# The first layer's experts in 40 steps instead of 47: whole tiles of one expert and mixed tiles of two experts' ends

## The reference

```python
# xn = layernorm(x): 1024 tokens x 256
logits = xn @ router_weight.T + router_bias            # 16 experts
top_val, top_idx = top_k(logits, 4)                    # 4 experts per token: 4096 rows in all
top_val = softmax(top_val)
gate_up = einsum('th,ehd->etd', xn, gate_up_proj) + gate_up_proj_bias   # per expert 256 x 512
gate, up = gate_up[..., ::2], gate_up[..., 1::2]
gate = minimum(gate, 7.0); up = clip(up, -7.0, 7.0)
glu = gate * sigmoid(gate * 1.702)
out = einsum('etd,edh->eth', (up + 1.0) * glu, down_proj) + down_bias   # per expert 256 x 256
out = (out * router_scores.T[:, :, None]).sum(axis=0)
x = x + attention(xn) * silu(out)
# second layer: linear attention, and 32 experts of 96 columns with a shared expert
```

## Time and profile before

| what | value |
|---|---|
| median of 3 runs | 425.56 us (424.31 to 426.42) |
| span of the profiled execution, first to last instruction | 422.5 us |
| what lies around the span, by the median | 3.06 us |
| PE busy | 407.8 us, 97% of the span |
| DVE busy | 330.4 us, 78% |
| first-layer tile loop on PE | about 39.0 to 176.5 us |

### The profile page before, as it was taken

The page is one execution under the profiler, slowest core; times in us unless marked ns, Lnnn a source line. Parts: engine busy times, 40 slices in busy tenths (PEclk is TensorE's granted clock), DMA queues, the critical chain, the costliest instruction groups (busy, mean ns, idle before and its releaser), DMA issues.

```text
span 422.5 us, 10072 instructions
## 1 busy us (share of the span) xinstructions
PE 407.8 (97%) x3213; PEld 321.5 (76%) x3213; DVE 330.4 (78%) x1121; ACT 233.1 (55%) x592; POOL 216.9 (51%) x208
## 2 busy tenths in 40 slices
PE   8999999999999999989999989999999999999995
PEld 4856999999999999856766668548877786565684
DVE  5876899999987666678999999847688774545896
ACT  3273233333433454589999972554777766633731
POOL 2114487888842322067786720067877740577710
PEclk9899999999999999969999999999999999999999
DMA  6947688889999998729977978023556553333322
GB/s 222 393 167 266 196 265 268 289 256 311 297 316 286 303 314 277 216 62 245 193 152 176 226 269 294 1 67 97 170 182 188 178 173 101 111 101 103 99 62 74
DMA packets 42275, 84.17 MB, mean 199 GB/s; under 512 B 7137, under 2 KB 27105, under 8 KB 41585
## 3 DMA queue, kind: packets, MB, share of 16 engines
q1 hardware_dynamic: 30656, 60.99, 44.1%
q0 software_dynamic: 9936, 20.85, 19.6%
q10 hardware_dynamic: 1632, 1.71, 1.2%
HBM read 65.81 MB, written 15.60 MB: 193 GB/s over the span
## 4 chain that ended last, share of the span: by engine, by line
PE 89%; DVE 7%; issue 2%; DMA 1%; ACT 1%; ACTq 0%; DVEq 0%
PE ps L1173 20%; PE ps L1189 9%; PE ps L1124 7%; PE ps L1370 7%; PE ps L1293 5%; PE ps L1151 5%; PE ps L1268 4%; PE ps L952 3%; PE ps L968 3%; PE ps L1381 3%; PE ps L1110 3%; PE ps L1162 2%; PE ps L971 2%; PE ps L941 2%; PE ps L1338 2%
## 5 line engine op out<-in xcount | busy, mean ns | idle before, releaser
L549 POOL DMA_INDIRECT til<-xn_rows,gidx x71 | 70.7, 996 | 86.4 <-PE ps L1162 38.9
L1173 PEld LDWEIGHTS ps<-til,experts 128*128 128x128 f32 x752 | 91.0, 192 | 3.7 <-issue 1.5
L1173 PE MATMUL ps<-til,experts 128*128 128x128 f32 x752 | 91.8, 275 | 0.1
L714 ACT ACTIVATE til<-ps 128x256 f32<-128x256 f32 x47 | 18.0, 383 | 69.8 <-PE ps L1162 69.8
L839 ACT ACTIVATE til<-til,mxs 128x128 f32<-128x128 f32 (+1 forms) x128 | 49.0, 452 | 0.0
L1189 PE MATMUL ps<-experts,til 128*128 x188 | 48.4, 381 | 0.0
L762 ACT ACTIVATE til<-ps,wtile 128x256 f32<-128x256 f32 x95 | 42.0, 468 | 3.7 <-PE ps L1153 2.4
L1795 DVE CUSTOM_DVE_ANT_0 til<-ps,cst 128x128 f32<-128x128 f32 (+1 forms) x128 | 37.8, 351 | 5.2 <-PE ps L1268 4.4
L1189 PEld LDWEIGHTS ps<-experts,til 128*128 128x128 f32 x188 | 32.1, 190 | 2.8 <-issue 0.3
L600 POOL DMA_INDIRECT rou<-sorted_rows,slotu x16 | 20.5, 1283 | 25.8 <-DMA sorted_rows<-til 19.4
L1126 PE MATMUL ps<-xn,til 128*64 128x192 f32 x192 | 33.8, 329 | 0.0
(11 more groups left out here) (247 smaller groups left out, 936.8 us busy)
## 6 DMA issues: line engine op xcount, KB each, us to landing
experts<-in_gu SPq DMA_DIRECT2D x47, 512.0 KB, 5.4
sorted_rows<-til SPq DMA_DIRECT2D x95, 128.0 KB, 1.9
experts<-in_gu SPq DMA_DIRECT2D x8, 768.0 KB
experts<-in_dn SPq DMA_DIRECT2D x4, 1024.0 KB, 12.4
experts<-in_dn SPq DMA_DIRECT2D x8, 384.0 KB
experts<-att SPq DMA_DIRECT2D x44, 32.0 KB
til<-xn_rows,gidx POOLq DMA_INDIRECT x71
xr<-in_x SPq DMA_DIRECT2D x2, 512.0 KB, 4.2
```

Of the source, the lines that this page charges most:

```text
L549: po.indirect_dma_start(to, None, xn_dram[s.n], bass.IndirectOffsetOnAxis(ap=gidx[:, t:t + 1], axis=0))\
L1173: mm = pe.matmul(ps[:, b0, m * P:(m + 1) * P], gw[:, j, k * w + m * P:k * w + (m + 1) * P], xgT[:, j % 2, k, :], start=(k == 0), stop=(k = ...
```

## The change

The first layer's experts are padded to 64 rows instead of 128. The whole pairs of 64 rows make 32 tiles of one expert (`WHOLE0`). What an expert has left over, at most 64 rows, is a half tile, and two of those stand side by side in each of 8 mixed tiles (`MIXED0`). The loop has 40 steps: four whole tiles with a mixed one as the fourth of each five. The weights lie in six slots (four in `big` and two in `att`), and a mixed tile fills two of them. It has its own path on each engine: the rows are the stationary operand, 64 columns of the array per expert; the bias comes in as a matmul; DVE gates rows instead of columns (`gate_rows`), PE turns the result back (`turn_rows_back`), ACT copies it (`copy_rows`), and ACT copies the second expert's down weights ahead (`copy_other_down`). The routing gets more DVE instructions. The fixed tile numbers are new: rotations after gathers 5, 8, 10, 13, 15, 18, 20 and 23, heads in SP's steps 14 to 24 and 25 to 35, the value columns after gathers 27 and 37, bias weights from tile 19, bias rows from 28. `weights_ahead` stays at five before the number of tiles, which is step 35 now. Some semaphores are merged into the engines' chains.

```diff
-NT0, NT1 = tiles_needed(E0, P), tiles_needed(E1, HALF_ROWS)
+NT0, NT1 = tiles_needed(E0, HALF_ROWS), tiles_needed(E1, HALF_ROWS)
+MIXED0 = E0 // 2
+WHOLE0 = NT0 - MIXED0
+STEPS0, MIXED_AT = 5, 3
...
+        gw = [big[:, n * 1024:(n + 1) * 1024] for n in range(4)] + [att[:, n * 1024:(n + 1) * 1024] for n in (6, 7)]
...
-        BIAS_TILE = 35
+        BIAS_TILE = 28
+        WEIGHT_TILE = 19
+        ROTATED = (5, 8, 10, 13, 15, 18, 20, 23)
+        HEADS_AT = (14, 25)
+        VALUES_AT = (27, 37)
...
 # SP
+                if i >= STEPS0:
+                    sp.wait_ge(L[0].gu_done, i - STEPS0 + 1)
+                for n, j in enumerate(slots_at(i)):
+                    if g == 0 and j == 4:
+                        sp.wait_ge(L[0].wide_done, NTT)
+                    e = sp.snap(halves[n] if mixed(i) else now[tile_at(i) % 4], min_val=0, max_val=E0 - 1)
+                    sp.dma_start(gw[j], gu0[:, bass.ds(e, 1), :].rearrange("p o n -> p (o n)")).then_inc(L[0].w_full[j], 16)
...
                     if s.n == 0 and t == s.NT - 5:
                         weights_ahead()
-                    if s.n == 0 and (16 <= t < 27 or 28 <= t < 39):
-                        place_heads(t // 28, t - (16, 28)[t // 28])
+                    for half, at in enumerate(HEADS_AT if s.n == 0 else ()):
+                        if at <= t < at + 11:
+                            place_heads(half, t - at)
...
 # POOL
-                    if s.n == 0 and t in (33, 44):
-                        a = t // 44
+                    if s.n == 0 and t in VALUES_AT:
+                        a = VALUES_AT.index(t)
                         po.wait_ge(s_heads[a], 16 * 32)
...
 # ACT
+                def copy_rows(i, j):
+                    if not mixed(i):
+                        return
+                    ac.wait_ge(s.rows_turned, i // STEPS0 + 1)
+                    ac.wait_ge(s.y_done, i - 1)
+                    ac.activation(hT[:, j % 2, :, :], ps[:, 4, 0:D].rearrange("p (k t) -> p k t", k=KD), ACT.Copy).then_inc(s.rows_copied, 1)
...
 # PE
+                    if mixed(t):
+                        h = 2 * tile_at(t)
+                        for c in range(2):
+                            pe.matmul(ps[c * HALF_ROWS:(c + 1) * HALF_ROWS, b0, :], selc[:, h + c:h + c + 1].broadcast_to([96, HALF_ROWS]), gub_bf, start=True, stop=False)
...
+                        for k in range(KD):
+                            for c, n in enumerate(slots_at(t)):
+                                rows = slice(c * HALF_ROWS, (c + 1) * HALF_ROWS)
+                                mm = pe.matmul(ps[rows, b0, :], xgT[:, j % 2, k, rows], gw[n][:, k * w:(k + 1) * w], start=False, stop=(k == KD - 1))
...
+                def turn_rows_back(t, j):
+                    if not mixed(t):
+                        return
+                    g = t // STEPS0
+                    pe.wait_ge(s.rows_gated, g + 1)
...
+                    for k in range(KD):
+                        mm = pe.transpose(ps[:, 4, k * P:(k + 1) * P], ubuf[:, j % 2, k * P:(k + 1) * P], ident)
+                    mm.then_inc(s.rows_turned, 1)
...
-                    run_tiles(s, [(1, 1, up), (0, 1, turn), (0, 4, experts), (0, 1, begin), (1, 1, weights), (1, 1, bias_rows), (3, 1, first_heads), (3, 1, down)])
+                    run_tiles(s, [(3, 1, turn_rows_back), (1, 1, up), (0, 1, turn), (0, 1, experts), (0, 1, begin), (1, 1, weights), (1, 1, bias_rows), (3, 1, first_heads), (3, 1, down)])
...
 # DVE
+                def gate_rows(t, j):
+                    ve.wait_ge(s.gu_done, t + 1)
+                    g, u = gbuf[:, j % 2, :], ubuf[:, j % 2, :]
+                    ve.tensor_scalar(g, ps[:, 2 + j % 2, 0:F], LIMIT, None, ALU.min).then_inc(s.g_ready, 1)
+                    ve.tensor_scalar(u, ps[:, 2 + j % 2, F:2 * F], 1.0, LIMIT + 1.0, ALU.add, ALU.min).then_inc(s.u_ready, 1)
+                    ve.wait_ge(s.u_ready, t + 1)
+                    link(ve.scalar_tensor_tensor(out=u, in0=u, scalar=1.0 - LIMIT, in1=g, op0=ALU.max, op1=ALU.mult))
+                    ve.wait_ge(s.sig_ready, t + 1)
+                    ve.scalar_tensor_tensor(out=u, in0=sig[:, j % 2, :], scalar=1.0, in1=u, op0=ALU.add, op1=ALU.mult).then_inc(s.rows_gated, 1)
```

More of the change, by code:

```diff
@@ L639, in _ @@
             second_owner = [ac.alloc_register(f"second_owner{j}") for j in range(4)]
+            other_owner = [ac.alloc_register(f"other_owner{j}") for j in range(2)]
             ac.wait_ge(s_dve, 1)
@@ L922, in _ @@
             before = [pe.alloc_register(f"expert_before{j}") for j in range(4)]
+            first_half = [[pe.alloc_register(f"first_half{g}_{j}") for j in range(2)] for g in range(2)]
             def turn(s, i):
@@ L1086, in tiles, with experts @@
                 gu, dn = gu1_sb, (dn0_sb, dn1_sb)[s.n]
-                def experts(g, j):
-                    if g > 0:
-                        for a, b in zip(before, now):
-                            pe.reg_mov(a, b)
-                    pe.load(now, texi[0:1, g * 4:g * 4 + 4])
+                def experts(i, j):
+                    g = i // STEPS0
+                    if i % STEPS0 == 0:
+                        pe.load((now, before)[g % 2], texi[0:1, g * 4:g * 4 + 4])
+                        pe.load(first_half[g % 2], texi[0:1, 2 * (WHOLE0 + g):2 * (WHOLE0 + g) + 2])
                 def experts_of_four(g):
@@ L1185, in down @@
                         pe.wait_ge(s_dn0, 80)
[L1186 to L1191 removed]
+                    g = t // STEPS0
+                    if mixed(t):
+                        pe.wait_ge(s.rows_copied, g + 1)
+                        e = pe.snap(first_half[g % 2][0], min_val=0, max_val=s.E - 1)
+                        for k in range(s.KF):
+                            pe.matmul(ps[0:HALF_ROWS, 6 + j % 2, 0:D], hT[:, j % 2, k, 0:HALF_ROWS], dn[:, bass.ds(e * (s.KF * D) + k * D, D)],
+                                      start=(k == 0), stop=(k == s.KF - 1))
+                            mm = pe.matmul(ps[HALF_ROWS:P, 6 + j % 2, 0:D], hT[:, j % 2, k, HALF_ROWS:P], dn_other[:, k * D:(k + 1) * D],
+                                           start=(k == 0), stop=(k == s.KF - 1))
+                    else:
+                        pe.wait_ge(s.h_ready, tile_at(t) + 1)
+                        e = pe.snap((now, before)[g % 2][tile_at(t) % 4], min_val=0, max_val=s.E - 1)
+                        for k in range(s.KF):
+                            mm = pe.matmul(ps[:, 6 + j % 2, 0:D], hT[0:s.FP, j % 2, k, :],
+                                           dn[0:s.FP, bass.ds(e * (s.KF * D) + k * D, D)],
+                                           start=(k == 0), stop=(k == s.KF - 1))
                     mm.then_inc(s.y_done, 1)
@@ L1454, in link, with mark @@
                 ve.wait_ge(s_dve, chain[0])
+            def mark(ins):
+                chain[0] += 1
+                ins.then_inc(s_dve, 1)
+                return chain[0]
+            done = {}
             def variances(s, h):
@@ L1923, in _ @@
               .then_inc(s_nmr, 1)
-            def mark(ins):
-                chain[0] += 1
-                ins.then_inc(s_dve, 1)
-                return chain[0]
-            done = {}
             def affine_scale(i):
```

235 lines of the change are left out of this document (143 added, 92 removed).

## The result

The changed kernel takes **440.65 us** (median of 4 runs, 439.13 to 444.79) against 424.94 us for the kernel before on the same chip (4 runs, 423.92 to 426.42). The ratio is 1.0384, with a 95% interval of 1.0327 to 1.0442: slower by 15.7 us. The forecast was 429.3 us with a range of 418.5 to 436, so the direction was right and the size was not. The profiled execution after has a span of 443.0 us at a mean clock of 0.964. It is the slowest of its four; the other three took 439.13, 439.36 and 441.95 us.

A forecast was written before the change was run, and what follows sets the result against it. PE was taken to bound the tile loop (busy 137.41 of 137.50 us), the DMA engines close behind. The terms -12.2 + 1.1 + 2.6 + 8.4 + 1.2 + 2.6 = +3.7 on 425.6 gave 429.3 us, range 418.5 to 436.

The forecast's parts named there:

- fewer tiles on PE: Tile loop: 32 whole tiles at 2.87 us and eight mixed at 3.9, plus smaller one-hot matmuls; -12.2 us in all.
- routing: Before the tile loop: additional DVE operations make the slots later, so PE's list moves by +1.1 us (0.5 to 1.6).
- wait at tile 28: First half: PE waits for a gather held behind POOL's wait for the heads; +2.6 us (0 to 4.5).
- wait at tile 38: Second half: PE waits for a gather held behind the last heads, which queue behind `weights_ahead`; +8.4 us.
- `copy_rows` on ACT: Tile loop: ACT's copies lie beside PE, with ACT 55 of 137 us in use; put at nothing.
- DVE under a rotation: Four mixed tiles meeting a rotation: slower DVE operations deliver gated rows late, 0.3 each; +1.2 us (0 to 3).
- clock: Steps behind the two waits for heads: PE runs at 1.2 GHz for a while; +2.6 us for both (0 to 6).
- D: Mixed tiles: 64-column matmuls of 512 columns do not overlap as those of 192 do; +22, 451 us; chance 0.03.
- B: Heads land within 2 us of issue; second wait 6.0 us, none at tile 28; -3.8, 421.8 us; chance 0.25.
- E: The waits at tiles 28 and 38 do not occur; 415.7 us; chance 0.12.
- C: Tile loop: DMA engines become the bound, ending near 326 GB/s; each wait grows 2 to 4 us; 434 us, chance 0.15.
- A: The forecast itself: waits for heads, above all the second, and the clock give the gain back; 429 us, chance 0.45.

The follow-up runs named there:

- e5: Changed kernel with three edits together: value products at 31 and 39, owners' numbers loaded once, first rotation behind gather 7; 414.44 us.
- e9: The changed kernel run again as it is, on the same chip as the run with fillers; 442.09 us.
- e5b: Changed kernel with the first rotation behind gather 7 instead of 5, the second and third moved by one gather each; 436.95 us.
- e4: Changed kernel with ACT loading the owners' numbers of all eight mixed tiles once, at the first tile; 437.31 us.
- e8: Changed kernel with filler transposes keeping PE at work through the gather waits of tiles 6, 28 and 38; 435.57 us.
- e1: Changed kernel with the value products of both halves placed later, at 31 and 39 instead of 27 and 37; 424.27 us.
- e6: Kernel before the change, with its second half's heads placed four turns later (32 to 42 instead of 28 to 38); 437.90 us.

## Why the forecast went wrong, step by step

| step | forecast | measured | from |
|---|---|---|---|
| fewer tiles on PE | -12.2 | -12.3 to -13.0 | e5's trace |
| routing | +1.1 | +0.2 | turn of tile 0 |
| wait at tile 28 | +2.6 | +4.4 | trace |
| wait at tile 38 | +8.4 | +8.6 | trace |
| wait at tile 6 | none | +2.6 (1.4 in e9) | trace, e5b |
| `copy_rows` on ACT | nothing | +7.7, of it 5.0 by the register load | trace, e4 |
| DVE under a rotation | +1.2 | inside the row above | e4 |
| clock | +2.6 | +6.5 (three gather waits) | e8 against e9 |
| sum | +3.7 | +17 to +18 | median: +15.7; e9: +17.3 |

**The step that failed** is the one that put ACT's copies at nothing: "ACT's copies (ACT has 55 of 137 us in use) lie beside PE". The busy share was right, 54.69 us after, and it was the wrong thing to read. What counts is the order in ACT's list. `copy_rows` stands behind `copy_other_down`, and that behind a register load that no busy time shows. PE turned the rows back at 89.48, ACT's tanh was over at 90.20 and its head transfer issued at 90.48, and the copy began at 92.36. It was priced neither with its duration nor with what stands ahead of it. The runs show 7.7 us of waits in its place, 5.0 of them by the register load (e4).

**The second failure** is a wait that the text did not look for. The change moved the first rotation from behind gather 7 to behind gather 5. DVE sets when it can start, 49.62 us before and 49.49 after; what changed is that POOL came to it two gathers earlier. It stood 6.97 us for DVE's line 1776 where it had stood 1.56, and the gather of tile 6 could start only at 54.12: 2.6 us of wait. The forecast followed the gathers behind the heads with this very reasoning and did not apply it to the rotations. The diff showed the number.

**The clock** had the right mechanism and the wrong size. The forecast took 6 us at 1.2 GHz behind one wait, worth 3. The profiled execution after has five such stretches in the loop by its windows of 2 us (60 to 62, 112 to 114, 140 to 144, 156 to 158 and 186 to 188 us); the medians give 6.5 us by the fillers. That is for three gather waits, so it cannot be set straight against the forecast's upper bound of 6 us for two. In the profiled execution, the slowest, it was more: outside its waits the loop took 161.26 - 15.6 - 7.7 = 138.0 us, and in e5 129.94 - 1.8 = 128.1, so some 9.8 us, an estimate.

**What held.** A mixed tile was put at 3.9 us. In e5, where nothing waits, a mixed `down` starts at 102.36 and the next at 117.69, so five tiles take 15.33 us and the mixed one 15.33 - 4 x 2.87 = 3.85. Pairs of 512 columns start 0.43 us apart (83.66 to 84.09), as scaled from the earlier trace rows, so D is out. Eight of 3.85 and 32 of 2.87 make -12.3 against the loop before; between the bounds above, e5 has 129.94 us with 1.8 of waiting, so -13.0.

The second wait is right in its main parts: release 11.2 us after the turn of tile 36 (forecast 10.8), PE at its turn after 6.5 (6.3), landed 2.7 after the gather's start. The last moves landed 5.2 us after their issue (176.97 to 182.19), not within B's 2 us. The first wait has its release 8.4 us after the turn of tile 25 (7.9) and PE at its turn after 10.4 (9.2), and is short by its gather: 5.2 us from issue to PE's turn (133.62 to 138.85) where 2.7 was taken from the second layer. In the loop, with weights under way, a gather takes longer: 4.6 us on the median from issue to landing in the loop after.

The routing's slots came 1.1 us later on DVE (20.74 to 21.81), not the 1.5 worked out, and the turn of tile 0 moved by 0.16 us only, so that chain did not set PE's time.

Rivals: B's gain needed the waits at tiles 28 and 38 together under 7.3 us, and E needed none; they were 13.0. C fell with e1 and e5, and its ceiling near 326 GB/s with it: from 100 to 110 us e5 moved 333 GB/s while PE was busy throughout. That the loop before never held more than 316 is true of stretches of 20 us only; cut into 40 slices of 3.5 us, it has one of 349. A, the forecast's own, was the mechanism for 13.0 of PE's 23.3 us of waits; its time was short by 11.4 us.

## What to carry to other kernels

For each wait that a change may add, read the list of the engine that is waited for from the awaited instruction backwards, and price what stands there: register loads and waits too, which no busy share counts. Count the steps between the last transfer and the tile whose gather waits for it: three and four were too few here, seven and eight were enough (the kernel before, e1). When a table of places moves, follow every entry on an in-order queue (here rotations as well as heads) by the same rule: what does it wait for, and who is queued behind it. And when PE is the bound, add to waits of some us about 0.4 of them again for the clock (6.5 us on 15.6 here, estimated from this kernel alone), or give PE something to do in it.

## What was not expected of the hardware

A load of two registers on ACT held the engine for 1.2 us: `copy_other_down` starts after 1.63 us of idle with it and after 0.43 us without it, at the same tile; over eight tiles the idle time differs by 0.84 us each. The Trainium skill, "DMA: Bandwidth & Descriptors" (Latency and other measured facts), gives about 0.6 us as the floor of a `tensor_load`, without a number of registers. If this load is one of that kind, both figures here lie above the floor.

Waits of one size did not always bring the clock down. In the changed kernel it was at 0.50 behind the 2.61 us at tile 6 and behind two of the waits for `copy_rows`, of 2.11 and 2.02 us. In e1, with 2.3 us at its longest gather wait and 7.6 us of `copy_rows`, the longest 2.3, it stayed at 1.00 in the loop. Why the same idle time counts in one place and not in another stays open.

In e6 the clock read 0.50 already within the wait, where PE did nothing (busy time of all engines from 172 to 180 us):

```profile
172.00:180.00 8.00, 0.00 (x0) 0.00 (x0) 0.00 (x0) 0.00 (x0) 2.88 (x4) 0.50 0.45 152
```
